# No stage barriers behind the choice of two experts, tile entries ahead of biases, and a last stage that adds through transfers

## What is computed

```python
# x: (16, 256, 256) after layer 0
def _L1_xattn_ref(Q, K):                       # stage 3
    scores = jnp.einsum('btd,bsd->bts', K, K) * mask[None]
    return Q + jnp.einsum('bts,bsd->btd', scores, Q)

def _L1_ffn_ref(x, Wg, bg, W1, b1, W2, b2, gamma, beta):
    logits = jnp.einsum('btd,de->bte', x, Wg) + bg          # 8 experts
    top2_vals, top2_idx = jax.lax.top_k(logits, 2)          # stage 3
    combine = jnp.einsum('btk,btke->bte', softmax(top2_vals), one_hot(top2_idx))
    h = gelu(jnp.einsum('btd,edh->bteh', x, W1) + b1)       # stage 4
    y = jnp.einsum('bteh,ehd->bted', h, W2) + b2
    out = jnp.einsum('bted,bte->btd', y, combine)
    return _layer_norm(x + out, gamma, beta)                # stage 5

x = x + _L1_xattn_ref(_layernorm(x), ctx)      # call this x3
x = x + _L1_ffn_ref(_layernorm(x3), ...)       # z = _layernorm(x3)
```

## Time and profile before

| | us |
|---|---|
| median of 3 runs | 1369.33 (1367.33 to 1369.45) |
| the profiled execution | 1379.14 |
| its span, first to last instruction | 1377.3 |
| stage 3, from its first transfer to the barrier behind it | 696.4 to 847.0 |
| barrier 3/4, until SP goes on | 847.0 to 852.3 |
| stage 4, PE from its first product of expert weights to the last | 864.8 to 1316.0 |
| barrier 4/5, until SP goes on | 1323.0 to 1327.4 |
| stage 5, from its first transfer to the end of the span | 1327.4 to 1377.3 |

### The profile page before, as it was taken

One profiled execution on the slowest core, in us unless ns is written; L12 is line 12 of the kernel. 1 busy time (PEld: TensorE's weight loads), 2 busy tenths in 40 slices (PEclk: granted clock), 3 DMA queues, 4 the chain that ended last, 5 costly groups with the idle time before them and its releaser, 6 DMA issues.

```text
span 1377.3 us, 24047 instructions
## 1 busy us (share of the span) xinstructions
PE 1145.9 (83%) x8296; PEld 1052.9 (76%) x8296; DVE 938.2 (68%) x2066; ACT 799.8 (58%) x1579; POOL 650.4 (47%) x581
## 2 busy tenths in 40 slices
PE   3889899898859999999948560999999999999920
PEld 2688778787648888888837450999999999999920
DVE  6667877876436666666347564678878788787848
ACT  3745666552325565555436520777787877778724
POOL 3434443333235666665424664354554544545347
PEclk8559998899979999999978775899999999999965
DMA  6543333211065666666369990233332333333256
GB/s 224 167 164 112 137 122 120 108 54 39 24 209 166 176 175 174 176 172 180 48 200 266 229 194 11 54 59 52 56 55 52 59 52 55 55 52 59 39 158 223
DMA packets 142313, 162.79 MB, mean 118 GB/s; under 512 B 29457, under 2 KB 122897, under 8 KB 140145
## 3 DMA queue, kind: packets, MB, share of 16 engines
q1 hardware_dynamic: 113120, 124.97, 29.8%
q0 software_dynamic: 27968, 35.48, 15.5%
q10 hardware_dynamic: 1104, 0.82, 0.2%
HBM read 117.36 MB, written 43.86 MB: 117 GB/s over the span
## 4 chain that ended last, share of the span: by engine, by line
PE 62%; DVE 13%; DMA 7%; issue 7%; ACT 5%; POOL 4%; POOLq 1%; SPq 1%; ACTq 0%; DVEq 0%
PE quad L1929 15%; PE pb L1948 12%; PE quad L1191 11%; PE pb L1206 6%; PE pb L354 4%; PE quad L300 4%; DMA c3T<-in_ctxT 4%; PE pb L368 3%; POOL dSL L1803 2%; DVE Dm L522 1%; PE pb L266 1%; ACT Dm L838 1%; POOLq L2230 1%; PE pb L1176 1%; PE quad L1910 1%
## 5 line engine op out<-in xcount | busy, mean ns | idle before, releaser
L1993 DVE TENSOR_TENSOR wl<-W,wh 128x1024 fp32r<-128x1024 f32 x156 | 188.4, 1228 | 86.4 <-ACT gl L2068 57.6
L2100 POOL DMA_INDIRECT dOUT<-y,es x71 | 135.3, 1905 | 219.8 <-DVE y L2025 210.1
L1948 PE MATMUL pb<-wh,hh 128*128 128x256 f32 x568 | 164.0, 289 | 0.0
L1948 PE MATMUL pb<-wh,hl 128*128 128x256 f32 x568 | 160.5, 283 | 0.0
L1948 PE MATMUL pb<-wl,hh 128*128 128x256 f32 x568 | 160.5, 283 | 0.0
L1332 POOL DMA_INDIRECT dACC<-ye,idxJ x64 | 100.6, 1572 | 103.6 <-ACT ye L1295 54.4
L2042 ACT CAST wh<-W 128x1024 fp32r x117 | 121.9, 1049 | 41.0 <-issue 29.1
L2068 ACT ACTIVATE gl<-quad,b1c 128x256 f32<-128x256 f32 (+1 forms) x312 | 124.7, 450 | 20.0 <-PE quad L1929 18.7
L1929 PE MATMUL quad<-xh,wh 128*128 128x256 f32 (+1 forms) x624 | 126.1, 284 | 6.7 <-ACT hh L2073 5.2
L1929 PE MATMUL quad<-xh,wl 128*128 128x256 f32 (+1 forms) x624 | 125.6, 283 | 0.0
L1929 PE MATMUL quad<-xl,wh 128*128 128x256 f32 (+1 forms) x624 | 125.6, 283 | 0.0
(11 more groups left out here) (282 smaller groups left out, 3202.7 us busy)
## 6 DMA issues: line engine op xcount, KB each, us to landing
MB<-dM SPq DMA_DIRECT2D x16, 1024.0 KB, 5.7
W<-in_W SPq DMA_DIRECT2D x16, 1024.0 KB, 10.8
wraw<-in_Wg SPq DMA_DIRECT2D x16, 512.0 KB, 6.5
wraw<-in_Wu SPq DMA_DIRECT2D x16, 512.0 KB, 8.0
wraw<-in_Wd SPq DMA_DIRECT2D x16, 512.0 KB, 5.3
b2c<-in_b SPq DMA_DIRECT2D x39, 128.0 KB, 3.2
xp<-in_x SPq DMA_DIRECT2D x16, 256.0 KB, 5.5
cT<-in_ctxT SPq DMA_DIRECT2D x16, 256.0 KB, 5.2
```

What stands on the lines that cost most here:

```text
L1948: ins = pe.matmul(bank.t[:, 0:256], a_[s][:, c, 128 * tt:128 * tt + 128], b_[n % 3][:, 256 * c:256 * c + 256], start=half == 0 and m == 0, ...
L1993: v.tensor_tensor(w_dst(wl[n % 3], kind), w_src(expert(i), kind, half), w_dst(wh[n % 3], kind), ALU.subtract).then_inc(*v_t.up("w", n))
L2100: g.indirect_dma_start(out=dOUT[:, :], out_offset=bass.IndirectOffsetOnAxis(ap=es[i % 6][:, tt, 1:2].bitcast(U32), axis=0), in_=y1[i % 2][ ...
```

## The change

- Barriers 3/4 and 4/5 are gone (`if n < 2`). In their place stand waits of single engines: SP waits for the entries (`sx_st`) and the table before it reads `te`; ACT waits for the first weights, for the stores of x3 and z and for the table before it touches a weight; SP waits for `sy_st` before it loads `zc`.
- `en`, `po` and `sx_st` are rings of three instead of two.
- The pieces of `W2` are issued at the end of steps 1, 2, 3 (pieces 0 to 2), 6, 7 (3 and 4) and 8 (5 to 7). SP no longer waits for them; ACT does before its third piece of weights. `gam` and `bet` are loaded behind them.
- x3 goes to `out` itself; `dX3` is gone.
- SP issues `es` two visits ahead of the biases, and `b1c` has a semaphore ring of its own, on which ACT waits before the first gelu of a visit.
- In visits 4 to 19 POOL issues one transfer each that adds beta (`bet`, 256 rows of 1 KB) to a block of `out` in memory.
- Stage 5 goes over eight pairs. All of `zc` stays in the core's memory. For the first ten blocks POOL adds the finished `nc` to `out` by an adding transfer of 256 rows; for the last six SP loads x3 plus beta back from `out` (`xc`), DVE adds it and SP stores. POOL adds no beta in this stage.

```diff
@@ memory of stage 3
-        en = M4.ring("en", 2, [128, 4, 2, 2])
+        en = M4.ring("en", 3, [128, 4, 2, 2])
-        sx_st = ring("slots_written", 2)
+        sx_st = ring("slots_written", 3)
@@ slots(p)
-                if p >= 2:
-                    v.wait_ge(*sx_st[p % 2].of(p - 2))
+                if p >= 3:
+                    v.wait_ge(*sx_st[p % 3].of(p - 3))
@@ sp_stage3
+            W2_AT = {1: (0,), 2: (1,), 3: (2,), PAIRS - 2: (3,), PAIRS - 1: (4,), PAIRS: range(5, E1)}
-                    sp.dma_start(by_chunk(dX3[pair_rows(j), :]), x2[j % 4][:, :, :]).then_inc(*x3_st[j % 4].up(j, by=16))
+                    sp.dma_start(by_chunk(out[pair_rows(j), :]), x2[j % 4][:, :, :]).then_inc(*x3_st[j % 4].up(j, by=16))
-                if at(i) is not None:
-                    sp.dma_start(W2[:, i, :, :], ...)
-            for s in (w1_ld, w2_ld, *x3_st, *z_st):
+                for x in W2_AT.get(i, ()):
+                    sp.dma_start(W2[:, x, :, :], ...)
+            sp.dma_start(gam[:, :], to_all(A["gamma"], D)).then_inc(*ln_ld.up("g", by=16))
+            sp.dma_start(bet[:, :], to_all(A["beta"], D)).then_inc(*ln_ld.up("b", by=16))
+            for s in (*x3_st, *z_st):
                 sp.wait_ge(*s.all())
@@ act_stage4
             def w_high(n):
+                    if n == 2:
+                        a.wait_ge(*w2_ld.all())
+            for s in (w1_ld, *x3_st, *z_st):
+                a.wait_ge(*s.all())
+            a.wait_ge(*v_r3.of("part tiles"))
             w_high(0)
-                            a.wait_ge(*es_ld[i % 6].of(i))
+                            a.wait_ge(*b1_ld[i % 6].of(i))
@@ pool_stage4
+            g.wait_ge(*ln_ld.all())
+                if 0 <= i - 4 < B:
+                    g.dma_start(by_chunk(out[rows(i - 4), :]), bet[:, :].unsqueeze(1).to_broadcast([128, 2, D]), accum_op=ALU.add
+                                ).then_inc(*beta_st.up(i - 4, by=16))
@@ sp_stage4
+            for s in sx_st:
+                sp.wait_ge(*s.all())
+            sp.wait_ge(*v_r3.of("part tiles"))
+            for i in range(VISITS + 2):
+                if i < VISITS:
+                    entries(i)
+                if i >= 2:
+                    biases(i - 2)
@@ dve_stage5
+            def scale(b):
+                n = nc_[b // 2 % 4][:, chunks(b), :]
+                v.wait_ge(*a_f.of("n", b))
+                v.tensor_tensor(n, n, gam[:, :].unsqueeze(1).to_broadcast([128, 2, D]), ALU.mult).then_inc(*v_f.up("g", b))
+                if b >= ADDED:
+                    v.wait_ge(*v_f.of("g", b))
+                    v.wait_ge(*fx_ld[(b - ADDED) // 2].all())
+                    v.tensor_tensor(n, n, xc[(b - ADDED) // 2][:, chunks(b), :], ALU.add).then_inc(*v_f.up("y", b))
+            for j in range(PAIRS + 1):
+                if j < PAIRS:
+                    stats(j)
+                if j:
+                    scale(2 * j - 2)
+                if j < PAIRS:
+                    shift(j)
+                if j:
+                    scale(2 * j - 1)
@@ pool_stage5
+            def add(b):
+                g.wait_ge(*v_f.of("g", b))
+                g.dma_start(by_chunk(out[rows(b), :]), nc_[b // 2 % 4][:, chunks(b), :], accum_op=ALU.add
+                            ).then_inc(*out_ad[b % 8].up(b, by=16))
+            for j in range(PAIRS):
+                s = fsm[j]
+                g.wait_ge(*v_f.of("v", j))
+                g.tensor_tensor(s[:, :, 8:9], s[:, :, 9:10], mhalf[:, :].unsqueeze(1).to_broadcast([128, 4, 1]), ALU.pow).then_inc(*g_f.up("r", j))
+                if 0 < j <= ADDED // 2:
+                    add(2 * j - 2)
+                    add(2 * j - 1)
@@ sp_stage5
+            sp.wait_ge(*sy_st.all())
             for b in range(B):
+                sp.dma_start(zc[b // 2][:, chunks(b), :], by_chunk(dOUT[rows(b), :])).then_inc(*fz_ld[b].up(by=16))
+            sp.wait_ge(*beta_st.all())
+            for b in range(ADDED, B):
+                sp.dma_start(xc[(b - ADDED) // 2][:, chunks(b), :], by_chunk(out[rows(b), :])).then_inc(...)
@@ tensor_program, vector_program, scalar_program, gpsimd_program, sync_program
-                if n < 4:
+                if n < 2:
                     end_of_stage(sp, n + 1)
```

More of the change, by code:

```diff
@@ L1862, in build @@
         es = M7.ring("es", 6, [128, 2, 2])
+        b1c = M7.ring("b1c", 6, [128, 8])
+        b2c = M7.ring("b2c", 4, [128, D])
+        wh = M7.ring("wh", 3, [128, 1024], FR)
+        wl = M7.ring("wl", 3, [128, 1024], FR)
         xh = M7.ring("xh", 2, [128, 2, TS], FR)
```

173 lines of the change are left out of this document (68 added, 105 removed).

## The result

The changed kernel took 1352.57 us (median of four executions, 1346.89 to 1356.42), the kernel before 1369.39 beside it (four executions). The ratio is 0.985, with a 95% interval of 0.982 to 0.987. Forecast were 1353.1. The sum was right to half a microsecond. Its terms were not, and most of what follows is about that.

The account below looks back on a forecast made before the run. Stage 4 was taken as PE-bound, stage 3 as limited by DMA, then POOL, with barrier relays and DVE in stage 5 behind. Gains of 4.4 + 6.1 + 0 + 4.3 + 1.4 = 16.2 us off 1369.3 gave 1353.1, range 1346 to 1363.

Parts of the forecast that it names:

- A: Stage 3, `W2` in parts: the last context load comes earlier, so the last entry lands 4.4 us earlier; bounds 0 to 8.
- the upper bound: Top of A's range in stage 3: 8 us, if the x of pair 7, awaited 3.70 us by POOL, comes earlier too.
- The pieces put last: `W2` pieces behind step 8 of stage 3: 3.1 MB in idle DMA time, cost nothing; without that cover 14 us.
- B: Between stages 3 and 4: barrier gone, 5.3 us, and entries loaded before biases, 0.8; together 6.1, bounds 5 to 7.
- C: Additions of beta in stage 4, covered by POOL's idle time: cost 0, up to 4 us if the cover failed.
- D: As a term: barrier 4/5 gone, 4.3 us gained. In formulas: POOL's time per stage 5 adding transfer, taken as 1.75 us.
- E: Stage 5 with POOL adding ten blocks: five periods of 5.25 us, POOL deciding; the stage gains only 1.4 us.
- T: Start of the first load of stage 5, forecast to move from 1327.4 to 1312.6 us.
- rival 1: Stage 5: adding transfers cheap (D up to 1.13), DVE decides, period 4.0 us; 22.4 us less, 1346.9; chance 0.17.
- Rivals 2 and 3: Stage 5 adding transfers dear: D 2.15 to 3.1, 1363.1 us, chance 0.14; or D 3.81, 1373.7, chance 0.06 (above 3.1).
- Rival 4: Stage 3: other traffic takes the moved piece's place, last context load no earlier; A is 0, 1357.5 us; chance 0.11.
- three signs of a wrong forecast: D outside 1.1 to 2.2; ACT waiting for buffers at pair 4; last `W2` pieces holding up ACT at stage 4's start.

Follow-up runs that it names:

- e1: The changed kernel again, nothing edited, as base of its series; 1360.0 us, ratio to the kernel before 0.987.
- e9: The changed kernel again, nothing edited, as base of a later series on another chip; 1361.6 us, ratio to the kernel before 0.987.
- e4: Changed kernel with `W2` pieces 3 to 5 at steps 5 to 7, `gam` and `bet` loaded in stage 4; 1360.8 us against 1360.0 unedited.
- e5: Changed kernel without the 16 adding transfers of beta in stage 4 (output lacks beta); 1350.7 us, no unedited kernel in its series.
- e8: Changed kernel with VectorE's shift in stage 5 placed behind both multiplications; 1354.1 us, stage 5 40.3 us.
- e2: Changed kernel with barriers 3/4 and 4/5 both put back; 1371.5 us against 1360.0 unedited, ratio to the kernel before 0.9945.
- e12: Changed kernel with the edits of e4 and e8 joined, beta additions kept away from half-width visits; 1353.9 us against 1361.6 unedited.
- e6: Changed kernel with each stage 5 adding transfer of 256 rows split into two of 128; 1356.7 us, stage 5 44.9 us.
- e3: Changed kernel with the `W2` pieces back at their earlier places, one per step 0 to 7; 1364.3 us against 1360.0 unedited.
- e10: The same edit as e3 again, in another series: `W2` pieces at their earlier places; 1361.2 us against 1361.6 unedited.
- e7: Changed kernel with four adding transfers in stage 5 instead of ten, VectorE adding pairs 2 to 7; 1357.7 us, stage 5 44.7 us.

## Why the prediction was right, and where it wasn't

**The sum** of the gains was forecast as 16.2 us; the medians moved by 16.8. Five terms carry it. That it came out within half a microsecond is luck, as the terms show.

**A**, 4.4 us forecast. The two first profiles show 7.2, and the mechanism as told: PE waited 5.4 us less for the last context load, and POOL rested nowhere after 777 us. The 4.4 is in them as the lost wait before z of pair 6, and the 2.8 more is what the upper bound named, x of pair 7. But the stage alone varies by 10 us between series, and on the two on which the pieces were put back the effect can't be told from nothing. If the steadier terms (-3.3 - 0.3 + 2.0 - 4.2 - 7.4 = -13.2) are taken from the 16.8 of the medians, 3.6 are left for A. The same subtraction with the stretches and medians of e1 leaves about 1, with those of e9 about -1, if the kernel before had the stretches of its one profile there too. That is an argument, not a measurement, and the size of A isn't settled. One reading of the prediction was wrong beside it: DMA was not nearly idle until 725 us. The share of 0.12 holds for 720 to 725 alone; from 700 to 710 it was 0.95, and over the whole stage 0.80. It bore on the place of piece 0, not on the sum.

**The pieces put last** were said to cost nothing, since "DMA had idled from about 824 on". This is the step that failed in B's neighbourhood. The idle DMA time was there, but 3.1 MB and two broadcast loads fill it, and the last entries share the DMA engines with them. As far as the pairing in e4 shows, that cost 3.1 us more to land in the first pair of profiles, 1.0 to 1.3 in e5 to e8 (5.6 to 5.9 us). No delay is seen only in the series where the stage ends 10 us later. I had priced the bytes against ScalarE's need of `W2`, not against the small transfers on the chain that share the engines, and the loads of gamma and beta, which the change put at the same place, weren't priced at all.

**B**, 6.1 us forecast: 6.3 between the profiles. e2 puts 5.0 of it on the barrier, and 1.1 to 1.2 on the order of entries and biases, which was given 0.8.

**C**, priced at 0 with up to 4: it is 2.0 in the first pair, and -0.1 to 2.0 by the other profiles against the same 451.2. POOL's time was covered as said; what I didn't look at was who else suffers. The cover was sought on the issuing engine alone, and the loss lay on ScalarE and PE at the half-width visits (e5, e12).

**D**, 4.3 forecast, 4.2 between the profiles, 5.4 in e2.

**E**, 1.4 forecast, 7.4 measured, the largest error. Three of its parts: the period 4.22 instead of 5.25 (5.2 us), the first period 1.1 us sooner (POOL's power of pair 1 at T + 8.4, not 9.5), the tail 13.1, not 12.8. The mis-sized term is D: 1.75 taken, 1.12 measured for 256 rows (e8), 0.80 for 128 (e6), where an indexed addition of 128 rows takes 1.55. Nor is there a 0.3 ahead of each transfer: POOL's own period is 3.62 where 1.75 + 2D would give 3.99. I took the addition's row as the nearest. What made it dear seems to be the index, as its direct neighbour without one costs half, and the direct additions of beta in stage 4, of 256 rows, took 1.38 there where the indexed ones of 128 took 1.63; but the two differ in their source too, and the index alone was not varied. The Trainium skill ("DMA: Bandwidth & Descriptors", section "Anatomy of one DMA — SWDGE (gpsimd) path") says that many descriptors come before their incremental cost shows; by that rule 128 and 256 rows would cost the same, and here they differ by 0.32 of 1.12 us.

With D below 1.13, **rival 1** was right about who decides: VectorE's loop. Its time of 1346.9 wasn't reached because of the two terms priced at 0: with 3.1 and 2.0 it is 1352.0. The forecast time came true since errors of +6.0 on one side and -5.1 on the other met. By the stretches of the first profiles, with the 2.8 more of A, it would be 1349.2. VectorE's period was put at 4.0 with a power's round trip of 1.2; it was 4.22, as the power takes 1.39 us beside VectorE's multiplications. The trace of the kernel before had that slowdown. Its power on half as many values took 0.7 us for the first two blocks, when VectorE had nothing to multiply yet, and 1.08 for the other fourteen:

```profile
1335.09 0.71 POOL L2199 TENSOR_TENSOR fsm<-fsm,mhalf 128x2 f32<-128x2 f32 x1 [1.44 <-DVE fsm L2158]
1337.13 1.08 POOL L2199 TENSOR_TENSOR fsm<-fsm,mhalf 128x2 f32<-128x2 f32 x1
```

Rivals 2 and 3 fall with D. Rival 4's A of 0 can't be excluded on the chips of e3 and e10, though not by its mechanism: PE's wait for the last context load did shrink, and the gain was lost behind it.

Of what the profile was to show: the gather stood 16.8 us earlier than at 857.1, but 6.4 of that are stages 1 and 2; PE in stage 4 is busy for 98% (446.1 us of the 453.5 from 847.5 on) and loses 2 us, so the share was too coarse a sign; an addition of beta cost POOL 1.38 us; DVE waits for POOL's power in each period as said, yet POOL also waits for DVE, which was the sign that the forecast of E was off. Of the three signs of a wrong forecast none came: D was 1.12, at the edge of the 1.1 to 2.2, and ScalarE was held up neither at pair 4 nor by the last `W2` pieces.

## What to carry to other kernels

A load that is moved off one wait lands on another: put a price on it also for the small transfers that share the DMA engines at its new place, and for each engine that works then, not only for the one that issues it. When a new operation has no row, vary the things in which it differs from its neighbours (here rows and index) one by one before taking the nearest row; and where two engines hand a small result back and forth in a loop, look for independent work to lie beside the round trip, as the second multiplication did (e8). Before reading a difference of one stage, profile the same code twice: here it varied by 10 us, more than any gain looked for. A sum that comes out right proves none of its terms: two errors of 5 and 6 us stood behind this one.

## What the runs showed of the hardware that I hadn't expected

- A direct adding transfer issued by POOL costs about 0.80 us of its time for 128 rows of 1 KB and 1.12 for 256 (from the periods of e6 and e8). With an index, 128 rows take 1.55 at least.
- POOL's power on 128 x 4 values takes 1.05 us with VectorE idle (pair 0), and 1.39 when VectorE multiplies a tile of 128 x 512 meanwhile, with or without transfers in POOL's queue (e7).
- The same stage of the same code took 138 to 141 us in the first profile and on one chip, and 148 to 150 on two others, while stage 5 repeated within 0.5 us everywhere.
- Sixteen adding transfers of 256 rows, spread over 170 us, lengthened PE's stalls at up to three visits where ScalarE is short of time by 0.5 to 0.6 us each; at other visits they cost nothing that shows (e5, e12).
